# A third of an edge pass's multiplication moved from VectorE to GpSimd

## The reference, cut to what matters

```python
q = (h @ Wq.T + bq).reshape(N, HEAD_DIM, HEADS) * scaling
k = (h @ Wk.T + bk).reshape(N, HEAD_DIM, HEADS)
v = (h @ Wv.T + bv).reshape(N, HEAD_DIM, HEADS)
s = jnp.einsum('edh,edh->eh', q[row], k[col])
m = jax.ops.segment_max(s, row, num_segments=N)
e = jnp.exp(s - m[row])
z = jax.ops.segment_sum(e, row, num_segments=N)
attn = e / z[row]
out = jax.ops.segment_sum(attn[:, None, :] * v[col], row, num_segments=N)
```

## Time and profile before

| | us |
|---|---|
| median of 3 runs | 7658.55 (7658.23 to 7661.41) |
| the profiled execution | 7664.92 |
| its span, first to last instruction | 7662.9 |
| from the first to the last L1486 of the pass | 781.35 |

### The profile page before, as it was taken

The page is one execution under the profiler, slowest core; times in us unless marked ns, Lnnn a source line. Parts: engine busy times, 40 slices in busy tenths (PEclk is TensorE's granted clock), DMA queues, the critical chain, the costliest instruction groups (busy, mean ns, idle before and its releaser), DMA issues. The chain is left out here.

```text
span 7662.9 us, 89136 instructions
## 1 busy us (share of the span) xinstructions
PE 5795.8 (76%) x21954; PEld 3657.7 (48%) x21954; DVE 4051.7 (53%) x9873; ACT 2728.5 (36%) x7590; POOL 3059.9 (40%) x3137
## 2 busy tenths in 40 slices
PE   5564677777995788876976788996888848997486
PEld 3332454443552566542545553553655525564243
DVE  7876456663112899965245334215566675556401
ACT  2534366661220344410114432111555515554010
POOL 1775444533772665610007750000455505553101
PEclk9999777677997877878988888897776666987597
DMA  2534211110001555510013330001333314333122
GB/s 89 159 91 146 53 31 37 37 24 27 2 2 42 167 160 159 159 35 13 0 57 106 105 71 23 0 0 42 85 87 93 93 41 112 98 98 80 56 101 73
DMA packets 268797, 547.49 MB, mean 71 GB/s; under 512 B 86992, under 2 KB 136588, under 8 KB 263948
## 3 DMA queue, kind: packets, MB, share of 16 engines
q0 software_dynamic: 134496, 314.63, 16.4%
q1 hardware_dynamic: 133932, 228.62, 9.5%
HBM read 493.99 MB, written 49.00 MB: 71 GB/s over the span
## 5 line engine op out<-in xcount | busy, mean ns | idle before, releaser
L1463 POOL DMA_INDIRECT L3a_edges_rows<-scratch_L3a,L3a_edges_index x416 | 404.4, 972 | 905.3 <-DMA L3a_edges_last<-order_dst_last 525.7
L1463 POOL DMA_INDIRECT L_edges_rows<-scratch_L_kv,L_edges_index x416 | 506.8, 1218 | 430.7 <-PE L_edges_ps_sum L1708 197.1
L632 POOL DMA_INDIRECT L_edges_rows<-scratch_L,L_edges_index x416 | 393.3, 945 | 572.7 <-SPq L616 446.3
L1463 POOL DMA_INDIRECT L_edges_rows<-scratch_L,L_edges_index x416 | 407.9, 981 | 530.4 <-DVE L_edges_msg L1510 293.6
L1463 POOL DMA_INDIRECT L3b_edges_rows<-scratch_L3b,L3b_edges_index x416 | 399.5, 960 | 393.2 <-PE L3b_edges_ps_sum L1708 225.4
L482 POOL DMA_INDIRECT scratch_by_dst<-dst_record,dst_dest x400 | 439.6, 1099 | 271.5 <-DVE dst_dest L334 150.1
L2505 DVE TENSOR_TENSOR L_experts_gated_h<-L_experts_hidden,L_experts_ps_g 128x800 f32<-128x800 f32 x112 | 110.6, 988 | 665.7 <-PE L_experts_ps_g L2458 665.7
L1584 DVE TENSOR_TENSOR L_acc<-L_edges_ps_sum,L_acc 128x264 f32 (+1 forms) x832 | 357.0, 429 | 156.9 <-PE L_edges_ps_sum L1708 91.9
L482 POOL DMA_INDIRECT scratch_by_src<-src_record,src_dest x400 | 383.1, 958 | 124.0 <-issue 121.7
L2496 ACT ACTIVATE L_experts_hidden<-L_experts_ps_h,L_eb_sb 128x400 f32<-128x400 f32 x320 | 190.2, 594 | 647.7 <-PE L_experts_ps_h L2451 647.7
L1708 PE MATMUL L3a_edges_ps_sum<-L3a_edges_rows,L3a_edges_hot 128*128 128x264 f32 x832 | 375.8, 613 | 2.1 <-DVE L_acc L1584 2.1
(11 more groups left out here) (771 smaller groups left out, 13174.8 us busy)
## 6 DMA issues: line engine op xcount, KB each, us to landing
x<-scratch_dst_key_rows SPq DMA_DIRECT2D x50, 512.0 KB, 4.6
x<-scratch_src_key_rows SPq DMA_DIRECT2D x50, 512.0 KB, 5.0
L_experts_w<-in_L_w SPq DMA_DIRECT2D x16, 1024.0 KB
L_edges_rows<-scratch_L,L_edges_index POOLq DMA_INDIRECT x832
L_edges_lo_rows<-order_src_lo_rows SPq DMA_DIRECT2D x52, 256.0 KB
L3a_edges_lo_rows<-order_dst_lo_rows SPq DMA_DIRECT2D x52, 256.0 KB
L3b_edges_lo_rows<-order_dst_lo_rows SPq DMA_DIRECT2D x52, 256.0 KB
x<-scratch_dst_lo_rows SPq DMA_DIRECT2D x50, 256.0 KB, 3.6
```

The costliest lines, as they stand in the source:

```text
L632: pool.indirect_dma_start(rows[:, n % RING, k, :], None, row_table, bass.IndirectOffsetOnAxis(index[:, t:t + 1].bitcast(U32), 0)).then_inc ...
L1463: pool.indirect_dma_start(rows[:, n % RING, k, 0:RW], None, row_table, bass.IndirectOffsetOnAxis(index[:, t:t + 1].bitcast(U32), 0)).then_ ...
```

## The change

In the second layer's pass VectorE multiplies only the first five tiles of a batch (`OWN` = 5) at L1566, and GpSimd multiplies the last three (`POOL_TILES` = 3) by a new instruction. GpSimd's stands in its queue behind the eight gathers of batch n and is for batch n-2. It waits for that batch's weights. TensorE waits for it ahead of the sum of tile 5, under a new semaphore. The last two batches' multiplications come after the loop, behind no gather. In the other passes `POOL_TILES` is 0.

```diff
+    POOL_TILES = 3 if kind == "dot" else 0
+    OWN = SB - POOL_TILES
...
+        weighed_pool = s.sem("weighed_pool")
...
             def _(pool):
+                def weigh_last(pool, c):
+                    pool.wait_ge(weighted, c + 1)
+                    out = parts(c)[:, OWN:SB, :, 0:V]
+                    nc.gpsimd.tensor_tensor(out, out, bcast(parts(c)[:, OWN:SB, :, V], V, 3), ALU.mult
+                                            ).then_inc(weighed_pool, 1)
...
+                    if POOL_TILES and n >= RING - 1:
+                        weigh_last(pool, n - (RING - 1))
+                if POOL_TILES:
+                    for c in range(NB - (RING - 1), NB):
+                        weigh_last(pool, c)
...
-                    out = parts(c)[:, :, act_heads:H, 0:V]
-                    scale = bcast(parts(c)[:, :, act_heads:H, V], V, 3)
+                    out = parts(c)[:, 0:OWN, act_heads:H, 0:V]
+                    scale = bcast(parts(c)[:, 0:OWN, act_heads:H, V], V, 3)
...
+                        if POOL_TILES and k == OWN:
+                            pe.wait_ge(weighed_pool, n + 1)
                         pe.wait_ge(merged, n * SB + (k + 1))
```

## The result

The changed kernel takes 7699.7 us (median of 5 runs, 7693.07 to 7706.38) against 7660.27 for the kernel before (5 runs, 7658.23 to 7669.0): ratio 1.0049, 95% interval 1.0036 to 1.0062. It is slower by 0.49%, outside the range 7622 to 7690, where I had forecast 7644. The rival "GpSimd gets in first" had 7685 and a chance of 0.25.

The account below looks back on a forecast made before the run. VectorE was taken to bound the short steps, with TensorE stretching the others. The terms -17.8 + 2 + 1.3 = -14.5 us, from the median 7658.6, gave 7644 us; range 7622 to 7690.

Parts of the forecast that it names:

- GpSimd gets in first: GpSimd's multiplication starts ahead of L1486 and delays it: 1.57 us lost for 0.81 won a step, 7685 us; chance 0.25.
- VectorE's shorter instruction: L1566 with 1280 elements takes 1475 ns, 0.81 us less; times 52 at most 41.9 us.
- TensorE lets 17.8 us through: Only the 22 steps where TensorE was idle ahead of its query pairs keep the 0.81 us each: 17.8 us.
- GpSimd's multiplication takes 1.5 us: GpSimd's new instruction on 768 elements, its two inputs read one after the other: 0.19 + 2 x 0.65 = 1.5 us.
- When it can run: VectorE's L1486 is 0.07 to 0.20 us ahead; GpSimd's multiplication waits, running 2.3 to 3.8 us into the step.
- The queue behind it and TensorE's new wait: Gathers queued later are paid by GpSimd's 3.8 us of waits a step; TensorE's wait, with 5 us cover, costs nothing.
- Ends, 2 us, and late multiplications in the scan, 1.3 us: Last two multiplications, behind no gather, coincide with VectorE's: 2 us; late ones running into scan L1522 now and then: 1.3 us.
- The exclusive lock: VectorE and GpSimd share ports, held for the full instruction by whoever starts first; a two-SBUF-input VectorE instruction takes part.

Follow-up runs that it names:

- five_only: Changed kernel with VectorE multiplying five tiles and nobody the other three, so the output isn't the reference's: 7645.31 us, ratio 0.9977.
- turn_between: Changed kernel with GpSimd waiting for the key multiplication and TensorE turning scores between the two later query pairs: 8713.52 us, ratio 0.9951; second time 7633.04 us, 0.9958.
- wait_for_keys: Changed kernel with GpSimd's multiplication also waiting until VectorE's next key multiplication is done: 7659.39 us, ratio 0.9993; second time 7658.34 us, 0.9985.
- gather_done_first: Changed kernel with a small memset, and a wait on it, between the gather and GpSimd's multiplication: 7661.67 us, ratio 0.9997.
- the memset: Changed kernel, but VectorE multiplies all eight tiles and GpSimd, in place of its multiplication, memsets used keys: pass 794.0 us, in a slower series.
- one_gather_later: Changed kernel with GpSimd's multiplication moved behind the first gather of the next batch in its queue: 7668.14 us, ratio 1.0004.
- null: Changed kernel with no tile given to GpSimd, the new semaphore still made and cleared: 7663.67 us against 7662.21, ratio 0.9996.
- before_turn_between: Kernel before the change, with only TensorE's turn of the scores moved between the two later query pairs: 7655.82 us, ratio 0.9986.

## Why the prediction was wrong

- **VectorE's shorter instruction**: right, 0.80 us saved for 0.81.
- **TensorE lets 17.8 us through**: right in size. 17 us with nothing on GpSimd (`five_only`), 17.6 in the pass where GpSimd waits. VectorE then waits 40 times at the scan, where I had 30 steps without room. That TensorE's order of work was the cap is shown by `turn_between`.
- **GpSimd's multiplication takes 1.5 us**: right, 1.48. The 4497 ns of the Trainium skill (GPSIMD Engine Reference, "Performance versus the Vector engine") scale, as an estimate, to 1.7 us, 15% too much here.
- **"When it can run"**: the step that failed. I took it that the multiplication comes behind L1486 and waits for it, because VectorE is ahead by 0.07 to 0.20 us in short steps and by more in long ones. It goes first in all 45 settled steps and L1486 (now L1501) is held instead. Two things were wrong. I put the multiplication 0.17 to 0.30 us behind the gather, from the gaps between two gathers and between two copies; neither row has an instruction of this kind behind a gather, and the gap is 0.01 to 0.02. With it GpSimd is 0.03 to 0.10 us ahead in 25 steps. And I took the start that a profile shows to decide: in 20 longer steps GpSimd starts up to 0.34 us later and still goes first, so the right gap alone would have foretold about half of the held time. `wait_for_keys` and `gather_done_first` show that nothing else was needed to undo the hold.
- **The queue behind it and TensorE's new wait**: right that they cost nothing. The list of waits of the changed kernel has no line in which TensorE waits for GpSimd ahead of a sum, and GpSimd still waits 146.4 us for TensorE's sums (197.1 before), so GpSimd is not the bound.
- **Ends, 2 us, and late multiplications in the scan, 1.3 us**: the first is right in size, 0.27 us at the last key multiplication and 1.9 at the first turn behind the pass (16.5 for 14.6). The second didn't occur in the changed kernel: no scan L1537 (L1522 before) is longer than 0.46 us, and before the longest was 0.50.
- **The rival "GpSimd gets in first"**: the right mechanism, with a price of 1.57 us a step where it happens. That price has the gap of 0.17 us in it, which the rival's own condition, under 0.10, excludes; with the gap of 0.02 it is 1.42. Measured are 64.2 us over 46 steps, 1.40 each, for 0.80 saved. It comes in nearly all steps, not in 31. And 0.25 was low: the forecast stood on a margin of 0.07 to 0.20 us, with gaps that were borrowed from other pairs of instructions.
- **The exclusive lock** (the Trainium skill, SBUF — State Buffer, "Who interferes with whom"): the traces agree that the whole instruction is held and that it takes a GpSimd instruction that reads (the memset holds nothing). That section gives the ports to the one that issues first. I took this for the start that a profile shows, and by that it agrees in `gather_done_first` and not in 20 steps of the changed kernel; when an instruction is issued the profile doesn't show.

The pass explains 20.0 us of a difference that is 28.3 in the profiled spans (7691.2 against 7662.9) and 39 in the medians. In the profiles another 6.6 us lie ahead of the pass (it begins at 2533.3 against 2526.7) and 6.5 between it and the first values multiplied in `L3a`; behind that 4.8 are won back. The scatter between runs is 13 us for the changed kernel alone.

Over all kernels there is a pattern. Where GpSimd multiplies, the median is 9 to 20 us worse than the pass says: 39.4 us slower for a pass 20.0 longer (changed kernel), 2.8 and 8.6 faster for 17.6 and 18.0 shorter (`wait_for_keys`, twice), 5.9 slower for 13.7 shorter (`one_gather_later`), 6.1 faster for 15.4 shorter (`gather_done_first`), 33.9 faster for 44.4 shorter (`turn_between`, second time). In the three others, `null`, `five_only` and `before_turn_between`, it is as the pass says or up to 5 us better. Each figure has some 7 to 10 us of uncertainty either way, so the pattern rests on all of them together. This cost seems to go with GpSimd's multiplication and not with the hold, which is gone in most of these. Some 2 to 3 us of it are the turn behind the pass; where the rest arises, no run here shows.

## What to carry to other kernels

Before giving elementwise work to GpSimd, list VectorE's instructions with two SBUF inputs near the place where it will run; one that it meets can be held for nearly all of GpSimd's instruction, so 1.5 us on GpSimd can cost more than the 0.8 us taken off VectorE. Fix the order with a semaphore, so that it runs beside a reduction or a PSUM read; don't rely on a margin of tenths of a microsecond, and don't borrow the gap behind one kind of instruction for another. And when an engine's shorter work is swallowed by a wait for another, try the other's order of work: here, on top of the split with its wait, this took 26.7 us more off the pass. Last, a gain in the stretch that was changed need not arrive in the whole: of 17.6 us, 3 and 9 did.

## What the runs showed of the hardware

- A gather is held as well: it ends 0.82 us after VectorE's two-input instruction, the same behind a shorter one (L1581 ends at 2922.67 and the gather of 2922.45 at 2923.50). Two SBUF inputs aren't needed for this: in the kernel before, 35 gathers end 0.82 us after an L1477, which compares one SBUF tensor with a scalar per partition (L1477 at 2914.92 takes 0.72 us, the gather of 2915.09 ends at 2916.45). Whether L1477 also meets a multiplication of GpSimd's, no run was made to show.
- VectorE's held instruction is shown as running. The hold doesn't appear as idle time or as a wait, only as a longer duration: 3.55 to 3.97 us for 2.28. The list of waits of the changed kernel has no line of VectorE's for it.
- GpSimd's multiplication, queued directly behind a gather, goes ahead of a VectorE instruction that is shown to start up to 0.34 us before it (20 of 20 steps). With a small instruction and a wait on it between them it doesn't (27 of 27 with VectorE 0.18 to 0.51 us ahead).
